# The value products of an attention loop follow their scores two key steps later, not three

## The reference

```python
q = (x @ Wq + bq).reshape(b, t, H, hd).transpose(0, 2, 1, 3)
k = ((x @ Wk + bk) @ Wl + bl).reshape(b, t, H, lhd).transpose(0, 2, 1, 3)
v = ((x @ Wv + bv) @ Wl + bl).reshape(b, t, H, lhd).transpose(0, 2, 1, 3)
attn = jax.nn.softmax(jnp.einsum('bhqd,bhkd->bhqk', q, k) * scale, axis=-1)
out = jnp.einsum('bhqk,bhkd->bhqd', attn, v)
out = out.transpose(0, 2, 1, 3).reshape(b, t, L)
return out @ Wo + bo
```

## Time and profile before

| what | us |
|---|---|
| time, median of 2 runs (4267.56 and 4304.87) | 4286.21 |
| the profiled execution's own time | 4264.57 |
| its span, slowest core (the cores: 4241.3 to 4263.0) | 4263.0 |
| PE busy | 2289.6 |
| DVE busy | 1551.9 |
| ACT busy | 1308.7 |
| DMA moved | 137.04 MB |

### The profile page before, as it was taken

One profiled execution on the slowest core, in us unless ns is written; L12 is line 12 of the kernel. 1 busy time (PEld: TensorE's weight loads), 2 busy tenths in 40 slices (PEclk: granted clock), 3 DMA queues, 4 the chain that ended last, 5 costly groups with the idle time before them and its releaser, 6 DMA issues.

```text
span 4263.0 us, 33363 instructions; the slowest of 8 cores (4241.3 to 4263.0 us)
## 1 busy us (share of the span) xinstructions
PE 2289.6 (54%) x9296; PEld 801.3 (19%) x9296; DVE 1551.9 (36%) x2164; ACT 1308.7 (31%) x1117; POOL 10.2 (0%) x16
## 2 busy tenths in 40 slices
PE   3777655655656554777655655656552333323333
PEld 1333211111111111333211111111111212111121
DVE  2444222322323223444222322323223445455545
ACT  0000155555555550000255555555550000000000
POOL 0000000000000000000000000000000000000000
PEclk9888878888888886888878888888886666666666
DMA  6000100000000002000100000000004221222221
GB/s 120 20 20 1 20 0 0 20 0 0 20 0 20 1 0 79 20 20 1 20 0 0 20 0 1 20 1 20 0 0 112 71 82 57 99 99 99 74 84 60
DMA packets 52842, 137.04 MB, mean 32 GB/s; under 512 B 7479, under 2 KB 7614, under 8 KB 52670
## 3 DMA queue, kind: packets, MB, share of 16 engines
q1 hardware_dynamic: 42206, 117.59, 7.7%
q0 software_dynamic: 10464, 17.32, 2.7%
HBM read 101.87 MB, written 50.33 MB: 36 GB/s over the span
## 4 chain that ended last, share of the span: by engine, by line
PE 35%; DVE 25%; ACT 24%; issue 7%; DMA 4%; DVEq 1%; ACTq 1%; SPq 1%; another core or an unknown queue 0%; POOL 0%; POOLq 0%
PE ps L324 14%; ACT pt_sb L484 12%; ACT xn_tok L484 11%; DVE xn_fm L523 10%; PE ps L878 3%; PE ps L422 3%; PE ps L529 3%; PE ps L499 2%; PE ps L467 2%; DVE xn_fm L521 2%; PE ps L502 2%; DMA xst<-z_scr 2%; DVE k_sb L910 1%; DVE pt_sb L622 1%; DVE pt_sb L678 1%
## 5 line engine op out<-in xcount | busy, mean ns | idle before, releaser
L521 DVE COPY xn_fm<-ps 1x1024 f32<-1x1024 f32 x64 | 78.0, 1219 | 1310.7 <-PE ps L502 1310.7
L484 ACT ACTIVATE pt_sb<-ps,cst_sb 128x1024 bf16<-128x1024 f32 x256 | 308.3, 1204 | 775.0 <-PE ps L471 734.3
L523 DVE RECIPROCAL xn_fm<-xn_fm 1x1024 f32<-1x1024 f32 x64 | 418.6, 6541 | 5.1
L529 PE MATMUL ps<-xn_fm,ones_sb 1*64 1x512 f32 x128 | 123.7, 1068 | 519.6 <-DVEq L166 519.6
L324 PE MATMUL ps<-xn_fm,arena 128*128 128x512 bf16 x1536 | 363.4, 401 | 27.8 <-DMA blrow_bf<-blrow 16.9
L467 PE MATMUL ps<-q_sb,k_sb 64*128 64x512 bf16 x512 | 227.8, 445 | 242.2 <-ACTq L166 205.9
L484 ACT ACTIVATE xn_tok<-ps,cst_sb 128x1024 bf16<-128x1024 f32 x256 | 308.3, 1204 | 82.1 <-issue 46.6
L484 ACT ACTIVATE pt_sb<-psT,cst_sb 128x1024 bf16<-128x1024 f32 x256 | 308.5, 1205 | 58.3 <-issue 58.1
L484 ACT ACTIVATE xn_tok<-psT,cst_sb 128x1024 bf16<-128x1024 f32 x256 | 308.5, 1205 | 54.1 <-issue 54.1
L467 PE MATMUL psT<-q_sb,k_sb 64*128 64x512 bf16 x512 | 221.2, 432 | 144.7 <-ACTq L166 140.1
L499 PE MATMUL ps<-xn_tok,vt_sb 128*65 128x512 bf16 x512 | 204.6, 400 | 75.3 <-ACTq L166 75.3
(11 more groups left out here) (142 smaller groups left out, 2671.6 us busy)
## 6 DMA issues: line engine op xcount, KB each, us to landing
xst<-x SPq DMA_DIRECT2D x32, 512.0 KB, 7.0
z_scr<-xst SPq DMA_DIRECT2D x64, 256.0 KB, 3.5
xst<-z_scr SPq DMA_DIRECT2D x64, 256.0 KB, 5.7
k_sb<-x SPq DMA_DIRECT2D x32, 512.0 KB, 8.3
x_scr<-q_sb SPq DMA_DIRECT2D x32, 512.0 KB, 2.6
k_sb<-x_scr SPq DMA_DIRECT2D x32, 512.0 KB, 5.3
out<-q_sb SPq DMA_DIRECT2D x32, 512.0 KB, 2.9
arena<-wq POOLq DMA_DIRECT2D x2, 2048.0 KB, 23.1
```

Of the source, the lines that this page charges most:

```text
L484: return sc.activation(pwide(pp), stb[pk][:, 0:1024], AF.Exp, bias=cst[:, 1:2], scale=cst[:, 0:1])
L521: v.tensor_copy(den_sb[0:1, :], av2[64:65, :])
L523: return v.reciprocal(rden[0:1, :], den_sb[0:1, :])
L529: t.matmul(drp[0:64, :], ones_r[0:1, 0:64], rden[0:1, 0:512], start=True, stop=True, tile_position=(0, 0))
```

## The change

One number: the value products come two key steps behind the scores, where they came three behind.

```diff
-                    AVLAG = 3
+                    AVLAG = 2
                     for tkc in range(16 + AVLAG):
                         if tkc >= AVLAG:
                             emit_av(tkc - AVLAG)
```

## The result

The changed kernel takes 4310.9 us (median of 11 runs, 4303.4 to 4348.1), the kernel before, on the same chip, 4269.3 us (median of 10). The ratio is 1.0133, with an interval of 1.0095 to 1.017. So it is slower by some 57 us (0.0133 x 4269), within the 2% that the prediction gave to "no change", and near the 53.6 us of its sum. The ratio leaves out the three slowest of the ten runs before as slowed ones, and none after, so its 57 us is more than the 41.6 us between the medians; the lowest runs lie 54.5 us apart. The forecast was 4318 us with a range of 4303 to 4343; 4310.9 lies in it, 7 us under the forecast.

A forecast was written before the change was run, and what follows sets the result against it. ACT bounds mid-pair and the reciprocal chain between pairs. 44 x 1.0 + 12 x 0.73 + 2 x 0.4 + 6 x 0 = 53.6 us on the profiled 4264.6 gives 4318 us, range 4303 to 4343.

The forecast's parts named there:

- What bounds the kernel: Mid-pair, ACT's exponentials 1.42 us apart; between pairs, the 6.54 us reciprocal; in six pairs with output projection, PE.
- Middle and end of a pair cost nothing: Mid-pair at full clock, 0.36 us of cover, so no cost; at the end of a pair, no cost either.
- The wait of av0: Pair start: av0 waits for L546 until 1.85 us after exponential 0 starts (X); exponential 2 comes 0.78 us late.
- The half clock: Pair start: PE at 1.2 GHz takes 0.99 us from value pair to scores, adding 0.15 a step; 1.0 us a pair.
- The hidden pause: 12 pairs of the second sequence: late scores hide ACT's 0.27 us pause before exponential 1, leaving 0.73 us a pair.
- The two first pairs: Pairs j = 0 of the first block: nothing to normalise before av0, so 0.4 us late each.
- The pairs with projection: Six pairs also carrying the previous block's output projection, where PE sets the pace: cost nothing, within 0.5 us each.
- the prediction's own sign: In the profile after: the forecast is wrong if pairs with output projection change by more than 0.5 us.
- The rule on the spacing of matmuls: Pair start: matmuls every N/1.2 ns, 0.85 us for two value products; exponential 2 0.64 us late, 4301 us total.
- the 148 us: Rival: attention's clock stays at half to the end of each pair, 2.7 us a pair, 4412 us; chance 0.08.
- come up early: Rival: clock already full when qk2 is reached, exponential 2 0.12 us late, 7 us in all, 4271 us; chance 0.12.
- No gain showed on ACT: Rival: exponentials on ACT wait less for value products that come a step earlier, 13 us gained, 4251 us; chance 0.03.

The follow-up runs named there:

- The late reciprocal: Kernel before, with denominators spread first and the reciprocal taken afterwards on 128 x 512 in place of L542: ratio 0.901 at lag 4, 0.925 at lag 3, 0.951 at lag 2.

## Why the prediction was right

Point by point, in the order of its steps:

- *What bounds the kernel.* ACT's pace in the middle of a pair, and the chain over the reciprocal between pairs. The late reciprocal confirms the second: with it out of that chain a plain pair is shorter by 6.7 us at lag 4 (34.09 to 27.42).
- *Middle and end of a pair cost nothing.* Right: lag 2 from step 8 on leaves 1105 and 1107 us.
- *The wait of av0.* L546 ended at X + 1.63, as read; the step to PE was 0.18 us, the lower of the two ends, so av0 came at X + 1.81 and not 1.85. Exponential 2 was 0.71 us late (forecast 0.78; in the seven plain pairs of the first query block it was 0.63), exponential 3 0.83 (0.89).
- *The half clock.* The passage from av0 to qk2 took 0.97 us (forecast 0.99). Where the clock rose ahead of step 4, the lateness stayed at 0.82 us; later rises made it 0.97 and up to 1.10 at exponential 15, by steps of 0.11 to 0.16 us (forecast 0.15 a step). The forecast's 1.0 us a pair came out as 0.95 in the 42 plain pairs, part of it (0.05) from a clock that fell before av15, which the prediction had only in its range.
- *The hidden pause.* 12 pairs of the second sequence: 0.81 us more (35.09 over 34.28), forecast 0.73; the other seven cores show 0.6 to 0.7.
- *The two first pairs*: 0.37 us, forecast 0.4.
- *The pairs with projection* are the one step that was off: forecast nothing within 0.5 us, measured 0.60 us on average (41.74 over 41.14), between -0.05 and 1.5. By the prediction's own sign, a change of more than 0.5 us, this step failed. PE's list is as long as before, as it says, but its time is not, since the time depends on when the clock rises: half clock lasted until X + 4.8 to 5.3 in the six pairs before and until X + 4.6 to 7.9 after, the projections begin at the same X + 1.9, and exponential 2 was 0.3 to 1.4 us late. That lateness stayed to exponential 15, and only some 0.3 us of it came back at the end of the pair.
- *The rule on the spacing of matmuls*, from the Trainium skill's page "TensorE: Matmul & The Clock Gate" (Back-to-back issue gap), would have put exponential 2 at 0.64 us late; it came 0.71 us late, 0.60 with the measured av0 put into that sum (1.81 + 0.85 + 0.61 + 0.16 - 2.83). The value pair and the change to the scores took 0.97 us and not 0.85: the rows decide for the trace.

The rivals: the clock came up in every pair, so the 148 us did not come. It did not come up early either; the run with 37 matmuls shows what that case would have been, 0.26 us a pair where 0.12 was forecast (av0 came 0.17 us later there than the forecast had it). No gain showed on ACT. The granted clock of the stages fell to 0.78 from 0.81 and 0.80, as forecast.

The sum of the steps, measured: 42 plain pairs 39.8 us, 12 with the pause 9.7, the two first 0.7, six with projection 3.6, which is 53.8 us without the last pair of each sequence; the forecast was 53.6. That they agree so closely is in part luck, as the pairs with projection added what the plain ones lacked. The forecast time of 4318 us lies 7 us above the measured median although its sum is no larger than the measured one; its base, the profiled execution before, had spent 15 us more in the first phase A than the one after.

## What to carry to other kernels

The lag between a producer and its consumer in a hand-written order has to cover the longest wait at the head of a loop, not only the steady state: count which instruction stands behind the first waiting one, and let work that another engine needs stand ahead of it. A longer lag than that brought nothing (1105 us a stage at lag 3 and at lag 4). The same wait made a pair 0.26 us late where PE was at full clock, and 1.0 to 1.3 us in most pairs where its clock had fallen in the idle time before. And a wait that is covered by a longer lag can be made longer on purpose: moving 6.5 us from the bare chain between pairs to 3.4 us under the lag was worth 10%.

## What the runs showed of the hardware

Filling the idle time with 30 unread matmuls (6.64 us of PE) did not keep the clock for what followed: 1.65 us of idle and the products L529 and L531 came behind them, and av0 ran at half clock (0.61 us). With 37 of them the same start ran at either clock, depending on the pair (0.38 or 0.61 us). The products L529 themselves became faster in both (0.61 us for 1.08), ACT's idle time ahead of exponential 0 fell from 11.54 us to 10.43, and a plain pair at lag 3 was 0.96 us shorter.

In the kernel before, the rise came at almost the same distance from X in pair after pair (X + 4.6 to X + 4.9 in the first sequence); after the change it wandered between X + 4.9 and X + 8.2. The lateness of a pair is therefore not one number but a small set of them (0.75 to 1.10 us at exponential 15 of the plain pairs).
